# Seven products instead of eight in the third sweep of a graph kernel, in 32-column tiles

## The reference

```python
h = relu(layernorm(x))
T1 = adj @ h
T2 = 2 * (adj @ T1) - h
T3 = 2 * (adj @ T2) - T1
x = x + h @ W[0] + T1 @ W[1] + T2 @ W[2] + T3 @ W[3] + bias0
h = relu(layernorm(x))
support = adj @ expmap(h)          # a scale for each node, with a tanh of its norm
x = x + logmap(support) @ kernel + bias1
```

## Time and profile before

| | |
|---|---|
| Median of 3 runs | 1854.3 us (1854.13 to 1854.94) |
| The profiled execution | 1854.24 us, its span 1852.4 us |
| TensorE busy | 1830.2 us, 99% |
| VectorE, ScalarE, GpSimd busy | 22%, 7%, 2% |
| Block loads | 626 of 1,024 KB, 91.5% of the DMA engines' time |

### The profile page before, as it was taken

The page is one execution under the profiler, slowest core; times in us unless marked ns, Lnnn a source line. Parts: engine busy times, 40 slices in busy tenths (PEclk is TensorE's granted clock), DMA queues, the critical chain, the costliest instruction groups (busy, mean ns, idle before and its releaser), DMA issues.

```text
span 1852.4 us, 22385 instructions
## 1 busy us (share of the span) xinstructions
PE 1830.2 (99%) x9620; PEld 825.3 (45%) x9620; DVE 413.7 (22%) x853; ACT 121.3 (7%) x233; POOL 41.1 (2%) x65
## 2 busy tenths in 40 slices
PE   7999999999999999999999999999999999999997
PEld 4444444444444445444444444344444444444444
DVE  7111111111122123000000001532321222122136
ACT  1000000000000000000000000311000000000014
POOL 0000000000000000000000000000000000000003
PEclk9999999999999999999999999999999999999998
DMA  9999999999999986888888785899999999999995
GB/s 379 421 421 421 421 420 416 387 394 389 399 371 381 374 331 228 319 295 298 295 302 304 263 303 208 331 379 377 372 383 395 384 377 382 407 384 384 406 397 202
DMA packets 94833, 662.31 MB, mean 358 GB/s; under 512 B 11408, under 2 KB 13712, under 8 KB 14608
## 3 DMA queue, kind: packets, MB, share of 16 engines
q1 hardware_dynamic: 93744, 660.64, 91.5%
q10 hardware_dynamic: 992, 0.23, 0.1%
HBM read 658.74 MB, written 2.10 MB: 357 GB/s over the span
## 4 chain that ended last, share of the span: by engine, by line
PE 97%; DVE 1%; DMA 1%; SPq 0%; issue 0%; ACT 0%; DVEq 0%
PE row_bank L523 36%; PE work_bank L503 19%; PE work_bank L537 17%; PE row_bank L492 12%; PE row_bank L525 4%; PE own_bank L553 3%; PE work_bank L505 3%; PE turned L608 2%; DMA ring<-adj_blocks 1%; PE work_bank L577 0%; SPq L417 0%; PE own_bank L564 0%; PE own_bank L608 0%; PE row_bank L608 0%; SPq L428 0%
## 5 line engine op out<-in xcount | busy, mean ns | idle before, releaser
L525 PE MATMUL row_bank<-ring,nodes 128*64 128x512 f32 x1728 | 756.6, 592 | 0.0
L523 PE MATMUL row_bank<-ring,nodes 128*64 128x512 f32 x1728 | 756.6, 592 | 0.0
L523 PEld LDWEIGHTS row_bank<-ring,nodes 128*64 128x64 f32 x1728 | 236.4, 137 | 419.0 <-issue 416.2
L505 PE MATMUL work_bank<-ring,nodes 128*64 128x512 f32 x936 | 420.8, 592 | 0.0
L503 PE MATMUL work_bank<-ring,nodes 128*64 128x512 f32 x936 | 420.8, 592 | 0.0
L537 PE MATMUL work_bank<-ring,nodes 128*64 128x512 f32 x1456 | 342.2, 592 | 0.3 <-DVE nodes L888 0.2
L492 PE MATMUL row_bank<-ring,nodes 128*64 128x512 f32 x1112 | 269.8, 596 | 6.2 <-DMA ring<-adj_blocks 6.2
L525 PEld LDWEIGHTS row_bank<-ring,nodes 128*64 128x64 f32 x1728 | 236.4, 137 | 0.0
L503 PEld LDWEIGHTS work_bank<-ring,nodes 128*64 128x64 f32 x936 | 127.9, 137 | 218.8 <-issue 218.8
L537 PEld LDWEIGHTS work_bank<-ring,nodes 128*64 128x64 f32 x1456 | 124.4, 137 | 169.6 <-issue 167.8
L784 DVE TENSOR_TENSOR partial<-partial,work_bank 128x512 f32<-128x512 f32 x148 | 101.7, 688 | 332.5 <-PE work_bank L537 331.4
(11 more groups left out here) (106 smaller groups left out, 518.4 us busy)
## 6 DMA issues: line engine op xcount, KB each, us to landing
ring<-adj_blocks SPq DMA_DIRECT2D x626, 1024.0 KB, 7.7
out<-resid SPq DMA_DIRECT2D x16, 128.0 KB, 1.9
resid<-x SPq DMA_DIRECT2D x7, 256.0 KB, 11.4
resid<-x SPq DMA_DIRECT2D x2, 128.0 KB, 3.5
w_raw<-cheb_weight ACTq DMA_DIRECT2D x2, 64.0 KB, 7.8
bias<-cheb_bias ACTq DMA_DIRECT2D x1, 32.0 KB, 2.8
bias<-hyp_bias ACTq DMA_DIRECT2D x1, 32.0 KB, 3.8
w_raw<-hyp_kernel ACTq DMA_DIRECT2D x2, 16.0 KB, 8.8
```

The source lines that it names most:

```text
L505: done = nc.tensor.matmul(bank[EVEN, :], nodes[:, c * C + k, B, :], data[:, k, :], start=k == 0, stop=k == C - 1)
L523: nc.tensor.matmul(bank[ODD, :], nodes[:, c * C + k, A, :], data[:, k, :], start=first and k == 0, stop=last and k == C - 1)
L525: done = nc.tensor.matmul(bank[EVEN, :], nodes[:, c * C + k, B, :], data[:, k, :], start=first and k == 0, stop=last and k == C - 1)
```

## The change

It concerns the third sweep. From row 6 on (`FAST_FROM`) a BOTH visit forms the 2 x 2 products of the feature block (two halves of the chunks, two halves of 32 features) with the adjacency block (two halves of the chunks, two halves of 256 columns) with seven products in place of eight. That needs four sums of the block's parts and four of the features' parts:

- VectorE makes three of the block's sums (T1 and T3 in one instruction, then T2) two visits ahead, into one of two buffers; GpSimd makes the fourth, T4, from T2.
- GpSimd makes the feature sums of a row (step SUMS) into another buffer, once for each row.
- The buffers are slots of the ring: 7 and 8 for the mixes, 9 to 12 for the feature sums. From visit 456 to the last fast visit, 692, blocks have the other seven slots.
- The seven products use tiles of 32 columns, four at different places at a time, 256 columns each. Their sums stand in both row banks, crosswise. A new step JOIN puts them together: five copies by ScalarE, some of them between groups of 32 partitions, and six additions by VectorE. The TURN of the row follows five visits behind the end of the row, not two.
- The AGAIN visits of level 4, the OWN visits and the TURNs of levels 3 and 4 use 32-column tiles too, in twice as many matmuls.

```diff
+MIX_SLOTS, SUM_SLOTS = (7, 8), (9, 10, 11, 12)
+FAST_FROM = 6
...
+        if level == 3 and row >= FAST_FROM:
+            follow(2 if row < NB - 1 else 1, ("JOIN", row), lambda: None)
+            visits_to_turn = 5
...
+    for i in fast:
+        mix_before.setdefault(in_order[in_order.index(i) - 2], []).append(i)
...
     for n, last in enumerate(last_visit_of):
+        if last > shared_from:
+            for k in MIX_SLOTS + SUM_SLOTS:
+                slot_free[k] = max(slot_free[k], shared_to)
...
+                for j in mix_before.get(i, []):
+                    n = mix_no[j]
+                    block, mixed = ring[:, slot_of[load_of[j]], :, :], ring[:, MIX_SLOTS[n % 2], :, :]
+                    pool.wait_ge(s_mixed, 2 * n + 2)
+                    nc.gpsimd.tensor_tensor(mixed[:, 2:4, N2], block[:, 2:4, N1], mixed[:, 0:2, N2], ALU.subtract)\
+                        .then_inc(s_fourth, 1)
...
+                    pe.wait_ge(s_sums, sums_no[c])
+                    pe.wait_ge(s_landed[slot], landed)
...
+                    rounds = [(("A11", "B11", 0, high, N1), ("A11", "B11", 1, high, N1)),
+                              (("A12", "B21", 0, low, N1), ("S3", "T3", 0, low, N2)),
+                              (("A12", "B21", 1, low, N1), ("S3", "T3", 1, low, N2)),
+                              (("S4", "B22", 0, low, N2), ("S2", "T2", 0, high, N2)),
+                              (("S4", "B22", 1, low, N2), ("S2", "T2", 1, high, N2)),
+                              (("S1", "T1", 0, high, N2), ("A22", "T4", 0, low, N1)),
+                              (("S1", "T1", 1, high, N2), ("A22", "T4", 1, low, N1))]
+                    for k, pair in enumerate(rounds):
+                        if k in (1, 3):
+                            pe.wait_ge(s_mixed, 2 * n + (k + 1) // 2)
+                        if k == 5:
+                            pe.wait_ge(s_fourth, n + 1)
+                        for part, (a, b, h, bank, columns) in enumerate(pair):
+                            for level in (A, B):
+                                lane = level * F + part * H
+                                done = nc.tensor.matmul(bank[lane:lane + H, columns], left(a, h, level), right[b][:, h, :],
+                                                        start=first and k < 2, stop=k == 6, tile_position=(0, lane),
+                                                        skip_group_check=True)
...
+                for j in mix_before.get(i, []):
+                    n = mix_no[j]
+                    block, mixed = ring[:, slot_of[load_of[j]], :, :], ring[:, MIX_SLOTS[n % 2], :, :]
+                    dve.wait_ge(s_visit, visit_no[fast[n - 2]] if n >= 2 else shared_from)
+                    dve.wait_ge(s_landed[slot_of[load_of[j]]], uses_of[load_of[j]] * 16)
...
+                if kind == "JOIN":
...
+                    dve.wait_ge(s_aside, 5 * row + 1)
+                    step(nc.vector.tensor_tensor(both, both, low[:, N2], ALU.add))
...
+                    dve.wait_ge(s_aside, 5 * (row + 1))
+                    nc.vector.tensor_tensor(joined[:, N2], both, aside[:, N2], ALU.add)
+                    nc.vector.tensor_tensor(own, high[:, N1], aside[:, N1], ALU.add).then_inc(s_cleared, 1)
```

## The result

The changed kernel takes 1909.8 us (median of 4 runs, 1902.2 to 1916.1) against 1854.2 us (1853.6 to 1854.9) for the one before: ratio 1.0298, 95% interval 1.0257 to 1.0338. It is slower by 55.5 us. The forecast of 1865 us had the direction, but a fifth of the size, and the time lies outside its range. The profiled execution of after is its fastest run, 1902.2 us; its trace therefore accounts for 48.0 of the 55.5 us (span 1900.4 against 1852.4).

The account below looks back on a forecast made before the run. TensorE, busy 99%, was taken to bound the kernel, with DMA close to its end. Terms +11.8 - 12.4 + 7.4 + 4 = +10.8 on 1854.24 us gave 1865 us, range 1830 to 1902.

Parts of the forecast that it names:

- (a): TensorE's products in the third sweep: a fast visit takes 3.03 us instead of 3.43; AGAIN stays at 1.72 us.
- (b): TURNs of levels 3 and 4: twice the matmuls at 29 ns a record, 0.93 us instead of 0.46, +7.4 us.
- (c): Block sums: VectorE's mixes take 1.22 and 0.69 us, GpSimd's T4 1.2 us; throughput is no trouble.
- (d): JOIN after each row: covered by the following visits; without cover up to 5 us ten times.
- (e): Seven-slot ring sets pairs at 5.33 us, not 5.15: 64 fast visits +11.8 us, the other 31 -12.4 us.
- the loop theory: With few slots, a slot's round trip (landing, mixes, T4, last two rounds, next load) sets the fast visit and AGAIN pair.
- L + 4.07: Least time of two pairs in the ring: landing L (issue to landing, taken as 6.6 us) plus mixes, last rounds, handovers.
- (f): The 31 AGAIN visits after row 15: the ring enters with few loads in hand, +4 us.
- PE or the DMA rate as the bound: Rival, third sweep: landing at or under 5.9 us, so the kernel gets faster, 1842 or 1820 us; 31%.
- Landing as slow as now: Rival, block loads: landing stays at 7.8 us, pair 5.94 us, kernel 1904 us; 12%.
- The loop and the gain cancelling: Rival, third sweep: landing between 6.1 and 6.4 us leaves the sum within 0.2%, 3.7 us; 13%.
- The tiles' failure: Rival, TensorE: four tiles don't run at once (over 2400 us) or each group drains before the next (2190 us); 4%.

Follow-up runs that it names:

- Experiments 2: The changed kernel with a fast visit's slot handed back after the fifth round and T4, not at the visit's end: 1887.3 us, 1.0176.
- experiment 3: The changed kernel with T4 made by VectorE behind its second mix in place of GpSimd: 1895.1 us, 1.0216.
- experiment 4: The changed kernel with GpSimd making T4 twice before it signals: 1959.0 us, 1.0568.
- Experiment 5: The changed kernel without the block's sums T1 to T4, TensorE multiplying unmixed parts in the same 28 matmuls: 1865.9 us, 1.0064.
- experiment 1: The kernel before, old products, with only seven of 13 slots for blocks between visits 456 and 692: 1880.9 us, 1.0142.
- 2 and 3 (9): The changed kernel with slots handed back after the fifth round and T4, and T4 made by VectorE: 1870.3 us, 1.0092.
- three edits: The changed kernel with reserved slots taken only while in use, slots handed back after the fifth round, and T4 by VectorE: 1846.7 us, 0.9965.
- Experiment 8: The changed kernel with 88 loads for single-product visits bringing only half their block's bytes: 1886.5 us, 1.0174.
- experiments 6: The kernel before with only 32-column tiles added in AGAIN of level 4, OWN and TURN: 1877.3 us, 1.0126.
- 7: The kernel before with 32-column tiles in every visit of the third sweep, BOTH too: 1855.1 us, 1.0004.

## Why the prediction was right in direction and wrong in size

**(a) The products: right.** Forecast 3.03 us, measured 3.02 (1608.87 to 1611.89); the four tiles run together, and the AGAIN stayed at 1.72.

**(b) TURN: wrong, by all of its 7.4 us.** I took the 29 ns a record of the earlier trace rows as the fastest pace of issue. It was the pace of two tiles. With four, a turn of level 3 in after is this:

```profile
1265.78 0.63 PE L743 MATMUL turned<-w_last,acc 128*32 128x64 f32 x32
1266.22 1.90 PE L667 MATMUL work_bank<-ring,nodes 128*32 128x512 f32 x16
```

32 records in 0.44 us, 14 ns each, where 16 took 0.46. The term is zero.

**(c) The sums: their lengths nearly right.** In the 54 visits with distance 4 the mixes took 1.24 and 0.71 us (forecast 1.22 and 0.69), GpSimd 1.30 (forecast 1.2, of ends 0.73 and 1.46). "Throughput is no trouble" was wrong for GpSimd's order: the feature sums of a row, which the forecast left out, held T4 back in six visits.

**(d) The JOIN: right.** It starts when ScalarE's first copy is there, and no one waited for the addition (L1015) that clears the banks:

```profile
L1015 DVE TENSOR_TENSOR common<-row_bank,aside x10: 415/418/424, 1262.5 to 1817.1; 128x256 f32<-128x256 f32 x10
its engine sat idle before it (us, times) until:
who waited for it (us, times):
busy tenths in 40 slices 0000000000000000000000000000000000000000
```

**(e) The ring: this step failed, by size.** The mechanism stands. Experiments 2, 3 and 4 change terms of the loop and little else; of the gain that the loop theory gave, 2 showed 0.80 and 3 showed 0.74, and 4's cycle grew by what was put in less what the landing gave back. Experiment 5 came out at the loop's figure. But I wrote that two pairs cannot be shorter than L + 4.07, with L = 6.6. Over the 54 visits the mean was, from the freeing visit's end: 0.02 to the issue, 7.08 to the landing, 0.18 until VectorE began, 1.24 and 0.71 with 0.03 between, 0.21 to GpSimd, 1.30, and 1.21 to the visit's end. That is 11.97, and 4.89 beside the landing, not 4.07. So 0.82 us of the missing 1.30 is in the rest and 0.48 in the landing. The 0.82 are these. The handovers are 0.3 us, not 0.1 (0.02, 0.09, 0.03, 0.08 and 0.06 in the usual visit). Another 0.2 is in no term of the forecast: in six visits GpSimd was at its feature sums when T4 could start, in eight VectorE was at other work when the block landed. The two last rounds take 0.28 more than the 0.87 of their starts, as the last record has to end. The lengths of the sums are the other 0.14. By half the cycle the pair would be 5.99; the mean of all 64, with the visits that have a distance of five or six, is 5.82: 64 x (5.82 - 5.15) = +43 us, against the forecast +11.8. The 31 other fast visits and all else in the stretch gave 4 us of the 12.4 expected, presumably since a shorter visit in front of a wait is lost in the wait. Together that is the 39.0 measured. Against the forecast's +10.8 the profiled execution has +48.0; of the 37 us between them the pairs are 31, the other fast visits 8, TURN -7, the end 3, and the time ahead of visit 478 is 2.

In L the fault was to choose it apart from the pair. The traces show that they hang together:

| kernel | cycle, us | L, us | mean pair, us |
|---|---|---|---|
| T4 twice (4), slower clock in part | 13.2 | 6.2 | 6.45 |
| after | 12.0 | 7.1 | 5.82 |
| T4 by VectorE (3) | 11.65 | 7.4 | 5.64 |
| slot back early (2) | 11.4 | 7.4 | 5.57 |
| small ring, old products (1) | 11.1 | 7.2 | 5.44 |
| 2 and 3 (9) | 10.9 | 7.5 | 5.38 |
| no sums (5) | 10.85 | 7.4 | 5.30 |

A landing of 6.6 us belongs to pairs of 6.1 to 6.2 us. At the pair that I forecast, 5.33, the landing is 7.4. The shorter the loop, the denser the loads and the slower each lands; the order is not strict, as experiment 1 shows. With L = 7.4 and my own rest of 4.07 the pair would have been 5.74, and the sum 1891 us, inside my range; the table has 7.1 to 7.4 for such a pair, and 7.1 gives 1881. A part of the rest could have been read: TensorE's last records last 0.16 us beyond their step in the earlier trace rows.

**(f) The end:** +6.9 us measured, +4 forecast. Experiment 1 has 5.8 of it without a single mix, so it is the ring that enters the tail nearly empty.

Where the 55.5 us are, then: small ring with the old products +26.7 (experiment 1); the fast products on it, with the small tiles and the JOIN, -15.0 (from 1 to 5); the block's sums +43.9 (from 5 to after). The kernel's own gain in the products was real, but could be taken only where the loop did not bind. **The rivals:** PE or the DMA rate as the bound (31%) did not come with this kernel, and did with three edits. Landing as slow as now, 12%, with 1904 us, comes nearest in number: its cycle of 7.8 + 4.07 = 11.87 is all but the measured 11.97. That is luck in part, since the landing in the loop was 7.1 and the rest longer. By the measure of the earlier trace rows, the median of all loads, the landing did stay nearly as slow, 7.6 against 7.8, so the sign "between 6 and 7.5 us" holds for the loop's loads alone. The loop and the gain cancelling (13%) needed L at 6.1 to 6.4. The tiles' failure (4%) is excluded by 3.02 us.

Left open: what the 7 us of landing consist of. Experiment 8 shows that half of the neighbour's bytes are 0.6 us of them; what makes up the rest between 4.7 and 6.4 was not taken apart. Nor was the part of experiment 1's 27 us that its loop does not explain. After's runs also lie 14 us apart where before's lie 1.3 apart. The slowest, 1916.1 us, has the lowest granted clock, 0.993 against 0.996 in the fastest; no experiment tells whether that is the reason.

## What to carry to other kernels

Space taken from a ring is paid in time of the round trip. Count for each slot how many visits lie between its release and its next use; once that is four, write the whole loop down, from release to release, with each handover, the last record's length, and what else stands in the same engine's order. Take the landing from a stretch with the same density of loads as the forecast itself gives, and go round until both agree. And when buffers are borrowed, borrow each only from its first write to its last read, hand blocks back at their last reader and not at the end of the visit, and keep the slower engine out of the loop: the same algorithm went from 3.0% slower to 0.35% faster by these three.

## What the runs showed of the hardware

**Changing the tile size costs TensorE 0.13 to 0.16 us** (experiments 6 and 7), while the size itself costs nothing at these shapes.

**TensorE's clock fell behind waits.** Each of the ten phases at 1.2 GHz in experiment 4 begins no more than 1.6 us from the end of a wait of 2.3 to 4.0 us, though not each such wait has one behind it. In after, where no wait of the stretch is longer than 2.0 us, the granted clock was 1.00 throughout.

**VectorE is held while GpSimd works.** In after, at 1664.58 us, GpSimd begins a T4, and an instruction of VectorE that begins 0.28 us later takes 1.27 us, where the same line takes 0.43 with nothing beside it:

```profile
1664.58 1.27 POOL L517 TENSOR_TENSOR ring<-ring 128x512 f32<-128x512 f32 x1 [5.49 <-DVE ring L922]
1664.86 1.27 DVE L862 SCALAR_TENSOR_TENSOR tmp<-small,resid 128x256 f32<-128x256 f32 x1
```

An addition of four elements a partition shows it most plainly. It begins 0.04 us behind a T4 and ends with it:

```profile
1670.55 1.28 POOL L517 TENSOR_TENSOR ring<-ring 128x512 f32<-128x512 f32 x1 [1.89 <-DVE ring L922]
1670.59 1.26 DVE L1069 TENSOR_TENSOR small<-roots,small 128x4 f32<-128x4 f32 x1
```

Nine of its 16 executions in after stand so and take 1.25 us; the five with no GpSimd instruction beside them take 0.16. Hence the means of the group in after and of the same line in the kernel with T4 by VectorE (experiment 3):

```profile
L1069 DVE TENSOR_TENSOR small<-roots,small 128x4 f32<-128x4 f32 x16 | 13.5, 843 | 0.5
```

```profile
L1066 DVE TENSOR_TENSOR small<-roots,small 128x4 f32<-128x4 f32 x16 | 3.1, 196 | 0.5
```

The Trainium skill states that GpSimd shares its SBUF interfaces with VectorE instructions that have two SBUF inputs (GPSIMD Engine Reference, "1. Specifications"). The trace agrees for this addition, with 1.25 us against 0.16. In the loop it weighed little: the first mix took 1.24 us where it counted.
